# A vision layer on one core: warming products, the order of the first loads, and the signals of the last tiles

## What is computed

```python
h = patchify(x) @ W_tok + b_tok                  # (576, 768) @ (768, 192)
h = layernorm(h + attention(h))                  # 12 heads of 64; q and k normalised over the heads' axis
logits = h @ Wr + br; top-2 of 8 experts, softmax of the two
gu = h @ Wgu + bgu; act = (max(up, -7) + 1) * gate * sigmoid(1.702 * gate)
ffn = sum over the two experts of weight * (act @ Wd + bd)
out = layernorm(h + ffn)
```

## Time and profile before

| | before |
|---|---|
| runs | 154.48, 154.60, 155.51 us |
| median | 154.6 us |
| profiled execution, its own time | 155.1 us |
| its span, first to last instruction | 153.3 us |
| PE, DVE, ACT, POOL busy | 143.9, 105.0, 96.0, 87.4 us |
| bytes read and written | 9.96 and 0.44 MB |

### The profile page before, as it was taken

How to read it: one execution, slowest core, us unless ns; L and a number is a source line. 1 busy time by engine, 2 the same in 40 slices (tenths; PEclk the granted TensorE clock), 3 DMA queues, 4 the chain that set the end, 5 groups by cost and what they waited for, 6 DMA issues and landing times. The chain is left out here.

```text
span 153.3 us, 3297 instructions
## 1 busy us (share of the span) xinstructions
PE 143.9 (94%) x1174; PEld 129.9 (85%) x1175; DVE 105.0 (68%) x255; ACT 96.0 (63%) x223; POOL 87.4 (57%) x101
## 2 busy tenths in 40 slices
PE   6999899999999899999989999999999999999950
PEld 2789899999965678888969889999998999999940
DVE  0035999169488798979786457688867685687662
ACT  3054987994497996857889976434468345344611
POOL 7701269490459568999798384549445244444312
PEclk9999999999999999999999999999999999999995
DMA  5999999800032000303300000000000000000012
GB/s 143 313 375 229 232 285 242 253 18 0 13 101 98 2 4 2 103 4 103 107 0 0 4 2 0 6 0 0 0 0 4 0 0 0 0 6 0 23 34 58
DMA packets 4543, 10.60 MB, mean 69 GB/s; under 512 B 624, under 2 KB 1456, under 8 KB 4528
## 3 DMA queue, kind: packets, MB, share of 16 engines
q1 hardware_dynamic: 4528, 10.41, 24.3%
HBM read 9.96 MB, written 0.44 MB: 68 GB/s over the span
## 5 line engine op out<-in xcount | busy, mean ns | idle before, releaser
L441 POOL TENSOR_TENSOR reg_r<-reg_q,reg_r 128x288 fp32r<-128x288 f32 x23 | 19.0, 831 | 21.4 <-ACT reg_r L682 21.4
L371 POOL TENSOR_TENSOR reg_w<-stage,reg_w 128x768 fp32r<-128x768 f32 x12 | 21.9, 1829 | 12.8 <-DVE reg_q L862 4.5
L682 ACT ACTIVATE reg_r<-reg_q 128x288 fp32r<-128x288 f32 x24 | 10.6, 443 | 24.9 <-DVE reg_q L1021 24.9
L1000 DVE TENSOR_SCALAR reg_q<-ps,bup 128x288 f32<-128x288 f32 x24 | 12.4, 516 | 6.7 <-PE ps L1234 6.4
L1230 PE MATMUL ps<-reg_r,reg_w 128*128 128x288 f32 x48 | 14.9, 310 | 0.0
L1231 PE MATMUL ps<-reg_r,reg_w 128*128 128x288 f32 x48 | 14.2, 295 | 0.0
L1234 PE MATMUL ps<-reg_r,reg_w 128*128 128x288 f32 x48 | 14.1, 295 | 0.0
L1232 PE MATMUL ps<-reg_r,reg_w 128*128 128x288 f32 x48 | 14.1, 294 | 0.0
L1233 PE MATMUL ps<-reg_r,reg_w 128*128 128x288 f32 x48 | 14.1, 294 | 0.0
L1021 DVE SCALAR_TENSOR_TENSOR reg_q<-reg_q 128x288 f32<-128x288 f32 x24 | 12.5, 522 | 2.2
L503 ACT ACTIVATE reg_w<-stage 128x768 fp32r<-128x768 f32 x13 | 10.9, 840 | 3.5 <-DMA stage<-w_qkv_a 1.6
(11 more groups left out here) (209 smaller groups left out, 461.0 us busy)
## 6 DMA issues: line engine op xcount, KB each, us to landing
reg_x<-xw_in SPq DMA_DIRECT2D x5, 416.0 KB, 6.3
stage<-w_gu_a SPq DMA_DIRECT2D x4, 384.0 KB, 6.0
stage<-w_gu_b SPq DMA_DIRECT2D x8, 192.0 KB, 3.7
stage<-w_qkv_a SPq DMA_DIRECT2D x3, 384.0 KB, 9.7
stage<-w_qkv_b SPq DMA_DIRECT2D x6, 192.0 KB, 9.5
stage<-w_down SPq DMA_DIRECT2D x3, 384.0 KB, 3.2
wout<-w_out SPq DMA_DIRECT2D x1, 576.0 KB, 12.6
out<-reg_q SPq DMA_DIRECT2D x6, 72.0 KB, 1.6
```

The costliest lines, as they stand in the source:

```text
L371: nc.gpsimd.tensor_tensor(dst[:, 1, :], raw, f(dst[:, 0, :]), ALU.subtract).then_inc(s_wlop, 1)
L441: nc.gpsimd.tensor_tensor(acts[:, n % NACT, 1], act_f[:, n % 4], f(acts[:, n % NACT, 0]), ALU.subtract).then_inc(s_alo, 1)
L1000: nc.vector.tensor_scalar(upw[:, n % 4], ps[:, e_bank(n) + 1, 0:TH], bup1[:, c:c + 1], LIMIT + 1, ALU.add, ALU.min).then_inc(s_u, 1)
```

## The change

Five edits. The warming products read a constant of ones that the program's preamble has written, so the wait for the memset is gone and the memset too, and there are eight of them. `NAT` is 2, so x2 goes in split form as well. ACT starts with an activation on one column (which puts the table load ahead) and then issues x1, x3 and x5; SP issues x0, x2 and x4. Tiles 3, 4 and 5 of the output have a semaphore each (`s_res1`), on which their stores wait, and the DVE scales wait no longer for the tile before.

```diff
-NAT = 3
+NAT = 2
...
+        s_res1 = [sem(f"s_res1_{i}") for i in range(3)]
...
-            for c in range(1, NC):
+            for c in (2, 4):
                 sp.dma_start(xs[:, c], xw_in[c]).then_inc(s_x[c], 16)
...
             for j in range(6):
-                sp.wait_ge(s_res, j + 1)
+                sp.wait_ge(*((s_res, j + 1) if j < 3 else (s_res1[j - 3], 1)))
                 sp.dma_start(out[TD * j:TD * j + TD, :], res[0:TD, j, :]).then_inc(s_out, 16)
...
-            nc.gpsimd.memset(filler, 0.0).then_inc(s_filler, 1)
...
         def _(act):
+            nc.scalar.activation(warm[:, :], nc.const_aps.tensor(1.0, [128, 1], f32), ACT.Copy)
+            for c in (1, 3, 5):
+                act.dma_start(xs[:, c], xw_in[c]).then_inc(s_x[c], 16)
...
                 nc.scalar.activation(res[0:TD, 3, :], ps[0:TD, Z_BANKS1[0], 0:D], ACT.Identity, bias=znb1[0:TD, :],
-                                     scale=zrstd[0:TD, 1, 0:1]).then_inc(s_res, 1)
+                                     scale=zrstd[0:TD, 1, 0:1]).then_inc(s_res1[0], 1)
...
                 dve.wait_ge(s_zr1, i + 1)
-                dve.wait_ge(s_res, 3 + i)
                 nc.vector.tensor_scalar(res[0:TD, 3 + i, :], z_tile(1, i), zmv[0:TD, 1, i, 0:1],
-                                        zrstd[0:TD, 1, i:i + 1], ALU.subtract, ALU.mult).then_inc(s_res, 1)
+                                        zrstd[0:TD, 1, i:i + 1], ALU.subtract, ALU.mult).then_inc(s_res1[i], 1)
...
+            ones = nc.const_aps.tensor(1.0, [128, BANK], bf16)
+
             def keep_warm(n):
 
                 for _ in range(n):
-                    mm(ps[:, 3, :], filler[:, 0:128], filler, start=True, stop=True)
-
-
-            pe.wait_ge(s_filler, 1)
-            keep_warm(6)
+                    mm(ps[:, 3, :], ones[:, 0:128], ones, start=True, stop=True)
+
+            keep_warm(8)
```

More of the change, by code:

```diff
@@ L113, in vit_layer @@
         h1 = reg_h[:, :].rearrange("p (a n) -> p a n", a=2)
-        filler = reg_h[:, 0:BANK // 2].bitcast(bf16)
         w2T = sb("w2T", [128, T], f32r)
@@ L192, in vit_layer @@
             sem(n) for n in ("s_small", "s_wo", "s_out", "s_rows", "s_onehot", "s_rawa", "s_lgb", "s_smlo", "s_xb", "s_w1hi", "s_w1lo")]
-        (s_filler, s_fill, s_sel, s_const, s_smprep, s_smhi, s_xhi, s_xlo, s_whi, s_wlod, s_wlop, s_tok, s_hthi, s_htlo, s_hb,
+        (s_fill, s_sel, s_const, s_smprep, s_smhi, s_xhi, s_xlo, s_whi, s_wlod, s_wlop, s_tok, s_hthi, s_htlo, s_hb,
          s_qk, s_sq, s_raw, s_ssq, s_ssk, s_fold, s_root, s_eps0, s_rec0, s_r0, s_nln, s_r, s_v, s_vev, s_qn, s_kn0, s_kn,
@@ L200, in vit_layer @@
             sem(n) for n in (
-                "s_filler s_fill s_sel s_const s_smprep s_smhi s_xhi s_xlo s_whi s_wlod s_wlop s_tok s_hthi s_htlo s_hb "
+                "s_fill s_sel s_const s_smprep s_smhi s_xhi s_xlo s_whi s_wlod s_wlop s_tok s_hthi s_htlo s_hb "
                 "s_qk s_sq s_raw s_ssq s_ssk s_fold s_root s_eps0 s_rec0 s_r0 s_nln s_r s_v s_vev s_qn s_kn0 s_kn "
```

## The result

| | before | after |
|---|---|---|
| median of 14 runs each, measured together | 155.44 us | 156.14 us |
| lowest and highest | 154.48, 156.61 | 155.81, 156.47 |
| profiled execution, its own time | 155.1 | 156.29 |
| its span | 153.3 | 154.5 |

The ratio is 1.0064, with a 95% interval of 1.0044 to 1.0085: the change makes the kernel slower by 0.4 to 0.9%, which is within the 1% that was called no change, but above the range of 153.7 to 155.1. Part of the distance is the base: over 14 runs the kernel before takes 155.44 us, not the 154.6 of its first three. The forecast was -0.3 us and the ratio says +1.0 (0.0064 x 155.4).

The account below looks back on a forecast made before the run. PE, busy 94% of the span, was taken to bound the kernel, with the data chain binding its front. Front 0.0 and tail -0.3 from the 154.6 us median gave 154.3 us, range 153.7 to 155.1.

Parts of the forecast that it names:

- front term: Start of the kernel, up to line 1258 at 18.22 us: taken as unchanged, 0.0, with bounds -0.3 and +0.75.
- ACT's issues, between 0.9 and 2.3: Start: x1 goes out at about 0.9 if ACT's sequencer passes the table load, at 2.3 if it waits.
- rival B: Start: x1 lands behind x2, at 7.9; front +0.28, time 154.6, or 154.75 with a late issue; chance 0.22.
- All bytes through weight piece 1 are the same, so piece 0 lands at 13.6: Start, weight loads: bytes set the landings, so weight piece 0 lands at 13.6 and piece 1 at 15.3 again.
- rival C: Start: two issuers feed the DMA engines earlier, filling holes; every landing and the front -0.3, time 154.0; chance 0.15.
- x2 at 7.9: Token embedding: x2 lands at 7.9, its low half is ready at 9.95, and tokens end at 15.87 against 15.82.
- The data chain binds: Front up to line 1258: weight piece 0 through ACT and DVE sets the pace; the token chain has 0.1 us slack.
- Rival D: Start: x5 lands near 13.3, not 11.2, delaying tokens and weight 0; front +0.75, time 155.05; chance 0.10.
- Rival E: Start: PE's clock rises at another moment, earlier or later; time 153.9 to 154.8; chance 0.08.
- Two native pieces: the saving is lost to the wait for x2: Token embedding: net -0.34 us on PE if operands were there, lost as x2 needs ACT and DVE after landing.
- PE has no wait over 0.6 us after line 1243: After the front: a front loss finds no gap to vanish in and is passed in full to the end.
- The tail, -0.3: Last output tiles: scales start earlier and the last output is issued 0.3 us earlier; bounds 0.0 and 0.35.

Follow-up runs that it names:

- e8: Kernel before with only the warming changed: eight products on the constant, from 0.84 us, no memset; 154.87 us, ratio 0.9995.
- e1: Changed kernel with x1 to x5 all issued by SP again, in order, on one queue; 155.7 us, ratio 1.0033 to before.
- e7: Kernel before with only the tail changed: own signals for tiles 3 to 5; 154.75 us, ratio 0.998.
- e5: Changed kernel with DVE's first memset (small_eps) done by POOL, one DVE instruction less; 155.6 us, ratio 1.003 to before.
- e10: Changed kernel, SP issuing x0's first half, x1, x3, x5, ACT x0's second half, x2, x4; DVE's first memset on POOL; 154.15 us, ratio 0.9936 to before.
- e3: Changed kernel with x2 and x3 swapped between queues: ACT issues x1, x2, x5, SP x0, x3, x4; 155.05 us, ratio 0.9978 to before.
- e9: Changed kernel with x2 issued second by ACT, x3 by SP, and DVE's first memset done by POOL; 154.6 us, ratio 0.9965 to before.
- e6: Kernel before with two more one-column memsets at the start of DVE's program; 155.67 us, ratio 1.0059.

## Why the prediction was wrong, point by point

The step that failed is the front term, taken as 0.0: it left x2's landing at 7.9 us. The runs showed x2 at 8.7 and the front at +0.80. Besides, the sum lacked a term, +0.55 in the middle, and stood on a base 0.8 too low.

- **The wait for the memset, nothing:** right. Products from 0.84, and e8 at 0.9995.
- **ACT's issues, between 0.9 and 2.3:** the lower bound holds. x1 goes out at 0.86, 0.06 us behind the start of a table load of 1.28 us. The sequencer passed it and x1 landed at 4.7, ahead of x2, so rival B had no ground. The Trainium skill (ScalarE: Activation LUTs, "What ACT_TABLE_LOAD costs") adds about 1380 ns of drain to each switch of tables. The trace does not bear that out: the issue did not wait, and the activation at 2.09 follows the load's end by 0.01.
- **"All bytes through weight piece 1 are the same, so piece 0 lands at 13.6":** wrong, in the kernel's favour. It took the bytes' rate as given, and two queues moved 399 GB/s between 3 and 5 us where one moved 286 in the profiled run of before and 265 in e1. Weight piece 0 came 1.5 us sooner. That is rival C's outcome, several times the 0.3 that its holes had been priced at, though not by holes: the DMA share was 1.00 between 3 and 5 us in before already. The rule that spoke against it (the Trainium skill, DMA: Bandwidth & Descriptors, "Issuing engines are not separate DMA queues") says that issuing from several engines only saves sequencer time. The traces differ from it at this place: between 3 and 5 us, with issued pieces waiting in the queue all the while, one queue moved 286 GB/s in before and two moved 399 in after.
- **x2 at 7.9:** the term that cost the most. The prediction took x2's landing over from before while it put x1, x3 and x5 in a queue of their own. If queues take turns, which it held likely, ACT's x3, issued at 1.27, goes ahead of SP's x2, issued at 1.73, and x5 (1.75) goes beside x2. It applied that to x1 and x5 and not to x2, nor to x0, whose parts came 0.8 and 1.5 later. x2 landed at 8.7, the tokens ended 0.95 later, and with 0.1 of slack the front was +0.80 rather than 0.0. Its own working, with x2 at 8.72, gives tokens at 15.87 + 0.8 = 16.7, within 0.1 of the trace. The chain was right, its input was not.
- **"The data chain binds":** true of before, and turned round in after: the data chain came 1.1 us early and the token chain bound.
- **Rival D** had the sign (the other side), but not the place: x5 was early (9.0); x2 was late.
- **Rival E**, the clock: it did rise early in this execution, and the eight native products' records start from 4.39 to 8.31, to end near 8.55 and not 9.24. PE then waits 0.96 for x2, so it gave nothing.
- **A reading of the earlier trace rows:** 37 GB/s between 1 and 2 us was taken as packets 0.8 us after an issue; nothing moves before 1.8, so it is 1.0. No term hung on it.
- **"Two native pieces: the saving is lost to the wait for x2":** right in kind. It is lost and more is.
- **The pause, +0.55:** in no step and no rival. "PE has no wait over 0.6 us after line 1243" was read as: a delay passes unchanged. It did, up to 98 us. That two more DVE instructions (the wait and the subtraction for x2) could move something 90 us later was not thought of.
- **The tail, -0.3:** right in mechanism. The last scale is -0.39; the stores take 0.2 of it back, as SP issues three in 1.25 us where the earlier trace rows had gaps between them (the last takes 0.42 in e7, against the 0.32 of tile 3 in before). Net -0.23, and -0.3 in e7.
- **Base and scatter:** 154.6 of three runs was 0.8 below the median of 14. The forecast's range should have held that; three runs from 154.48 to 155.51 said so.

## What to carry to other kernels

When loads are dealt to two queues, write down the landing order that turn-taking gives and lay it beside the order of use; a piece that needs further engines after it lands must not come last. Between the deal of the change and the deal in order of use lay 1.5 us here (e5 against e10), with the same bytes, queues and engines. A change in the number of instructions of an engine can show far from where it is made: if a step appears where the diff touches nothing, look for idle time without a releaser and move it with one instruction more or less. And the longest wait in a profile can be worth nothing, if what follows it waits for data.

## What the runs showed of the hardware that was not expected

- **One queue moves less at the start.** Between 3 and 5 us the five kernels with one queue moved 236 to 286 GB/s (e8 lowest, before highest) and the eight with two 394 to 406. The DMA engines' busy share was 0.84 to 1.00 with one and 1.04 to 1.07 with two, so for the most part it is the packets that took longer, and not engines that stood idle. Why was not tried. From 7 to 9 us the difference is small (378 in before, 407 in after).
- **What lies behind lands sooner, but not more steadily.** ACT takes weight piece 0 between 13.03 (e8) and 14.33 (e1) in the five traces with one queue, between 10.88 (e3) and 12.34 (e9) in the eight with two.
- **A pause at a fixed position of an engine's stream,** before record 192 of DVE and of ACT, and on DVE 128 records further on: 0.46 us of idle time on DVE and 0.37 on ACT with no releaser. It shows where nothing else makes the engine wait (the critical instruction in after, e1, e3 and e6) and is hidden in the others behind a wait for PE of 0.85. A packet of the instruction queue starts 0.65 to 0.69 us after the paused instruction of these four. That the fetching of instructions is the cause fits all of this and is not proven.
- **DVE and POOL slow each other by order of start:** line 1021 takes 0.46 when it starts 0.09 ahead of POOL's product, and that product then 1.03; with POOL's first it takes 0.83, and POOL's 0.80.
- **The clock's rise moves.** Line 1208's 16 records (0.24 apart at the 2.4 GHz level, 0.48 at 1.2) start from 4.4 to 8.3 in after, all at the higher level but for two waits, and from 4.4 to 9.0 in e3, whose program on PE is the same; so the rise lay before 4.7 in one execution and near 6 in the other. In before and e7, which differ in the tail alone, it lay near 6.4 and 5.5. It is worth up to 0.6 us of native products here and belongs to the execution, not to the kernel; the profile prints a granted clock of 1.00 throughout.
